# Second attention: x's sum for six of eight batches moved from VectorE to GpSimd

## The reference, cut to what matters

```python
# x = x + _L1_xattn_ref(_layernorm(x), ctx, ctx, Wq, Wk, Wv, Wo)
q = (queries @ Wq).reshape(b, s, KV_HEADS, GROUP, HEAD_DIM)      # 8, 4, 16
k = (keys @ Wk).reshape(b, s, KV_HEADS, HEAD_DIM)
v = (values @ Wv).reshape(b, s, KV_HEADS, HEAD_DIM)
scores = jnp.einsum('bqhgd,bkhd->bhgqk', q, k) * scale
attn = jax.nn.softmax(scores, axis=-1)
out = jnp.einsum('bhgqk,bkhd->bqhgd', attn, v)
return out.reshape(b, s, EMBED) @ Wo
```

## Time and profile before

| | us |
|---|---|
| median of 3 runs (lowest, highest) | 1831.98 (1831.41, 1835.54) |
| profiled execution, its own time | 1834.82 |
| its span, first to last instruction | 1833.1 |
| TensorE busy in the span | 1771.9 |
| VectorE busy | 1412.0 |
| ScalarE busy | 664.4 |
| GpSimd busy | 661.2 |
| mean granted TensorE clock | 0.992 of full |
| six batches of the loop, 1004.4 to 1084.1 | 79.7 |

### The profile page before, as it was taken

The page is one execution under the profiler, slowest core; times in us unless marked ns, Lnnn a source line. Parts: engine busy times, 40 slices in busy tenths (PEclk is TensorE's granted clock), DMA queues, the critical chain, the costliest instruction groups (busy, mean ns, idle before and its releaser), DMA issues. The chain is left out here.

```text
span 1833.1 us, 29590 instructions
## 1 busy us (share of the span) xinstructions
PE 1771.9 (97%) x10246; PEld 1503.6 (82%) x10246; DVE 1412.0 (77%) x2869; ACT 664.4 (36%) x1810; POOL 661.2 (36%) x447
## 2 busy tenths in 40 slices
PE   8999999999999999998998998899999999999998
PEld 6888899889888898896876764685888888888886
DVE  7767777777777777777547966888878888888886
ACT  5432232233331231234046765630443433343333
POOL 6633333444433433433121003544432433243331
PEclk9999999999999999999999998999999999999999
DMA  4111101011111111111023212020110111011011
GB/s 175 63 52 51 50 23 51 31 51 51 51 51 51 39 34 41 41 45 40 22 57 95 64 34 69 23 65 11 37 46 24 46 34 34 23 37 43 24 35 46
DMA packets 45034, 85.35 MB, mean 47 GB/s; under 512 B 5968, under 2 KB 23568, under 8 KB 44592
## 3 DMA queue, kind: packets, MB, share of 16 engines
q1 hardware_dynamic: 44976, 84.59, 14.7%
HBM read 75.39 MB, written 2.10 MB: 42 GB/s over the span
## 5 line engine op out<-in xcount | busy, mean ns | idle before, releaser
L658 POOL TENSOR_TENSOR l0x_comb<-l0x_neg,l0x_bias 128x1024 f32<-128x1024 bf16 x32 | 70.1, 2191 | 370.8 <-DVE l0x_probs L1061 358.6
L953 ACT ACTIVATE l0x_probs_t<-bank 128x512 f32<-128x512 f32 x32 | 19.1, 597 | 494.1 <-PE bank L795 494.1
L2959 POOL TENSOR_TENSOR l3x_q<-l3x_q,l3x_cross 128x512 f32<-128x512 f32 x64 | 89.8, 1408 | 188.0 <-DVE l3x_q L1920 188.0
L37 PE MATMUL bank<-l0x_w_v_hi,ctx_hi 128*128 128x256 f32 x512 | 144.9, 283 | 0.0
L39 PE MATMUL bank<-l0x_w_v_hi,ctx_lo 128*128 128x256 f32 x512 | 144.9, 283 | 0.0
L38 PE MATMUL bank<-l0x_w_v_lo,ctx_hi 128*128 128x256 f32 x512 | 144.9, 283 | 0.0
L937 ACT ACTIVATE l0x_probs<-l0x_probs,l0x_top 128x129 f32<-128x129 f32 x256 | 99.4, 391 | 49.4 <-DVE l0x_top L1067 49.4
L3146 ACT ACTIVATE l3x_probs<-l3x_probs,l3x_top 128x128 f32<-128x128 f32 x256 | 99.1, 389 | 38.1 <-DVE l3x_top L3227 38.0
L37 PE MATMUL bank<-ctx_hi,l0x_w_k_hi 128*128 128x512 f32 x256 | 104.0, 406 | 8.0 <-DVE ctx_lo L1145 8.0
L1107 DVE TENSOR_TENSOR x<-x,bank 128x512 f32<-128x512 f32 x120 | 82.0, 683 | 37.6 <-PE bank L39 37.6
L37 PE MATMUL bank<-l3x_qin_hi,l3x_w_q_hi 128*128 128x512 f32 x256 | 105.8, 413 | 2.2 <-ACT l3x_v L3180 1.9
(11 more groups left out here) (486 smaller groups left out, 5307.0 us busy)
## 6 DMA issues: line engine op xcount, KB each, us to landing
l0x_raw_k<-L_k_dram SPq DMA_DIRECT2D x32, 256.0 KB, 3.4
l0x_raw_v<-L_v_dram SPq DMA_DIRECT2D x16, 512.0 KB, 3.3
l0x_raw_q<-L_q_dram SPq DMA_DIRECT2D x16, 512.0 KB, 4.3
l0x_raw_o<-L_o_dram SPq DMA_DIRECT2D x16, 512.0 KB, 3.4
l3x_raw<-L_q_dram SPq DMA_DIRECT2D x16, 512.0 KB, 3.3
l3x_raw<-L_o_dram SPq DMA_DIRECT2D x16, 512.0 KB, 3.2
kv_raw<-L_kv_dram SPq DMA_DIRECT2D x8, 512.0 KB, 3.4
l1x_stack<-ctx_hi SPq DMA_DIRECT2D x56, 64.0 KB, 2.1
```

Source lines behind the costliest of these rows:

```text
L37: pe.matmul(out, lhs[0], rhs[0], start=start, stop=False)
L658: pool.tensor_tensor(comb[:, :, :], neg[:, :, :], bias[:, j:j + 1, :].to_broadcast([P, B, P]), ALU.add).then_inc(comb_ready, 1)
L953: act.activation(probs_t[:, 0:BH, :], bank[6][:, :].rearrange("p (b n) -> p b n", b=BH), ACT.Copy).then_inc(t_act, 1)
L2959: pool.tensor_tensor(dst[:, part], dst[:, part], cross[n][:, :], ALU.add).then_inc(rotated, 1)
```

## The change

For the first six batches, ScalarE copies bank 7 to a new tile `projected` (two slots in SBUF) behind the exponential of phase 3, and raises `copied`. GpSimd adds that tile to x and raises `o_done`. TensorE's second half of the value product waits for `copied` instead of `o_done` in batches 1 to 6. VectorE takes the statistics of batch b-1 in phase 0 of batch b, behind the division, once `o_done` says that x is there. ScalarE's copy waits for the sum of two batches before, whose slot it takes.

```diff
+    BY_POOL = B - 2
+        projected, copied = sb("projected", [P, 2, D]), sem("copied")
...
                 pool.wait_ge(q_full, 2 * G)
-                ffn.gpsimd(pool)
+                def add_out(b):
+                    pool.wait_ge(copied, b + 1)
+                    pool.tensor_tensor(x[:, b, :], x[:, b, :], projected[:, b % 2, :], ALU.add).then_inc(o_done, 1)
+                ffn.gpsimd(pool, add_out, BY_POOL)
...
-                    wait(pe, at_done if h == 0 else o_done, b)
+                    wait(pe, at_done if h == 0 else copied if b <= BY_POOL else o_done, b)
...
+                def copy_out(b):
+                    act.wait_ge(o_full, b + 1)
+                    wait(act, o_done, b - 1)
+                    act.activation(projected[:, b % 2, :], bank[7][:, :], ACT.Copy).then_inc(copied, 1)
...
                     act.activation(probs[u % 2][:, :, :], probs[u % 2][:, :, :], ACT.Exp).then_inc(exp_done, 1)
+                    if u >= 9 and (u - 9) % G == 0:
+                        copy_out((u - 9) // G)
                     if u >= 5 and (u - 5) % G == 0:
                         copy_values((u - 5) // G)
...
                         if phase == 0:
                             divide(b)
+                            if b >= 1:
+                                dve.wait_ge(o_done, b)
+                                ffn.norm.spread(dve, b - 1)
                         if phase == 1:
                             result_low(b)
-                        if phase == 3:
-                            add_out(b)
...
-    def gpsimd(self, pool):
+    def gpsimd(self, pool, add_first, by_pool):
         pool.memset(self.ones[:, :], 1.0).then_inc(self.ones_done, 1)
         for b in range(B):
+            if b < by_pool:
+                add_first(b)
             self.norm.root(pool, b)
```

## The result

The changed kernel takes 1843.53 us (median of 11 runs, 1842.16 to 1845.51), the kernel before 1833.49 us in 11 runs of the same comparison (1830.84 to 1842.42). The ratio is 1.0054, with an interval of 1.0046 to 1.0063: about 10 us slower (8.4 to 11.6). Forecast were 10.5 us and 1842.5 us.

The account below looks back on a forecast made before the run. VectorE was taken as the bound, with TensorE deciding once per batch through bank 7. Late release 0.93 plus moved statistics 0.82 gave 1.75 us, times six 10.5, on 1831.98: 1842.5 us, range 1838.5 to 1847.

Parts of the forecast that it names:

- The bound: Second attention pass: VectorE sets the pace, except once per batch, at unit 0, where TensorE does, 0.1 us apart.
- rival "faster": Unit 0 doesn't wait for bank 7, so VectorE's sum decides: 0.71 us less per batch, 4.3 us, 1827.7 us; chance 0.04.
- The release of bank 7: Value product's second half waits for ScalarE's copy behind unit 3's exponential: 0.93 us later per batch, bounds 0.9 to 1.1.
- The spared 1.53 us do nothing: Addition and statistics leaving VectorE before unit 0's maxima gain nothing; VectorE then stands idle some 2.6 us.
- The moved statistics: Behind the next batch's division on VectorE, they cost their whole 0.82 us per batch; bounds 0 to 0.82.
- The lower bound of 0: Low limit for the moved statistics' cost per batch, if VectorE waited at unit 1 anyway.
- rival "statistics free": VectorE waits at unit 1 anyway, so only the late bank release costs: 5.6 us, 1837.6 us; chance 0.08.
- GpSimd: Its sum into x, median 1.29 us, ends before the statistics start, with at least 2.2 us of cover.
- The sum: Late release plus moved statistics, 0.93 + 0.82 = 1.75 us per batch, six batches: 10.5 us, giving 1842.5 us.
- The clock: TensorE's clock stays 1.00 in the stretch although it is busy only 83%; a fall would show the prediction wrong.
- the rival with 0.05: TensorE's clock falls in the loop; one batch wholly at 1.2 GHz gives 1852 us, more than one more; chance 0.05.
- The rule on a saturated VectorE: Skill's advice that handing work from saturated VectorE to ScalarE or GpSimd may pay; predicted not to hold at unit 0.

Follow-up runs that it names:

- e5: The kernel before without VectorE's first six additions of the output product to x, nothing waiting for them: 1831.17 us, ratio 0.9994 to the kernel before.
- e1: The kernel before plus a ScalarE copy behind unit 3's exponential, for which the value product's second half also waits: 1838.34 us, ratio 1.0031 to the kernel before.
- e3: The changed kernel with ScalarE's copy of bank 7 ahead of unit 3's exponential instead of behind it: 1837.89 us, ratio 1.0026 to the kernel before.
- e2: The kernel before with only the statistics moved behind the next batch's division, addition left on VectorE: 1838.09 us, ratio 1.0025 to the kernel before.
- e6: The changed kernel with two more sums on GpSimd ahead of each sum into x: 1843.29 us, ratio 1.0059 to the kernel before.
- e7: The changed kernel with four more sums on GpSimd ahead of each sum into x: 1854.70 us, ratio 1.0118 to the kernel before.
- e4: The changed kernel with the copy ahead of unit 3's exponential and statistics between unit 0's maxima and subtraction: 1830.80 us, ratio 0.9993 to the kernel before.

## Why the prediction was right

*The bound.* Right: TensorE through bank 7 and VectorE were 0.1 us apart at unit 0. e5 is the test: with the addition gone VectorE just waits longer. One thing under the rival "faster" was wrong: it held that VectorE's sum decides once bank 7 is free by 1031.6, 0.1 us earlier. In e5 nothing holds bank 7, and VectorE still waits 0.64 us at unit 0: behind the bank comes TensorE's own queue (both halves of the value product, then the transposes), which ends only 0.29 us earlier than before.

*The release of bank 7.* Forecast 0.93 us, measured 0.98 to the subtraction of unit 0. The copy was shorter (0.58 us for 0.60), and TensorE's weights came 0.11 us after its end instead of 0.05. e1 shows the step alone, e3 that the place behind the exponential is its whole cause: ahead of it the same copy brings the subtraction of unit 0 to 3.81 us, as without any addition (e5).

*The spared 1.53 us do nothing.* Right: VectorE waits 2.71 us at unit 0, forecast some 2.6.

*The moved statistics.* 0.82 us in full, as forecast, and 0.80 alone in e2. The lower bound of 0 and the rival "statistics free" are refuted.

*GpSimd.* The sum has 1.27 us and is covered by 3.3 us, where I had at least 2.2; e6 and e7 fix the point from which it decides.

*The sum.* 1.75 us per batch forecast, 1.79 measured. From the subtraction of the first unit 3 to that of the last unit the two profiled executions take 74.14 and 85.38 us, 11.24 more: 6 x 1.79 = 10.74, and 0.5 that one fall of the clock costs, in the period that is 15.56 instead of 15.07. Their spans differ by only 8.3 us. Ahead of this stretch the changed kernel is 0.7 us later, and behind it the kernel before takes 3.7 us longer. There its clock fell at 1105 to 1110 (0.66) and 1320 to 1330 us (0.96 and 0.70) and the changed kernel's, about 10 us later, did not; these three windows make up to 3.4 us, an estimate from the missing share of the clock. So the two spans are no clean measure, and the medians, 10.0 us apart, are the better one. The 1842.5 us are 1.0 off: the kernel before came out 1.5 us above the median that they start from, and the difference 0.5 below the forecast. The 3 us taken for the spread of its runs were small; its first three runs already span 4.1.

*The clock.* The sum has no fall of the clock in it, and the prediction lists one as a sign of being wrong. In the profiled execution there was one: the rival with 0.05 came true in a small form, not a whole batch at 1.2 GHz but part of one, and its 0.5 us are too little to move the result. Windows of the changed kernel:

```profile
1050.00:1055.00 5.00, 3.94 (x33) 2.22 (x34) 2.28 (x3) 3.33 (x4) 1.27 (x1) 1.00 0.00 0
1055.00:1060.00 5.00, 3.46 (x30) 2.95 (x28) 4.70 (x8) 2.82 (x5) 1.06 (x3) 1.00 0.33 80
1060.00:1065.00 5.00, 5.00 (x21) 4.20 (x22) 4.29 (x5) 3.97 (x5) 0.00 (x0) 0.66 0.34 82
```

TensorE was busy 3.46 of 5 us ahead of the fall. e3 has a like one in the loop (its third and fourth period are 14.32 and 14.73), and e7 one in every batch but the first, with TensorE busy 1.52 and 1.32 of 4 us ahead of the two shown. The Trainium skill, "TensorE: Matmul & The Clock Gate", What's actually happening, has the throttled clock as the default which activity lifts. e7 fits this, as its clock fell behind stretches with little work on TensorE, at 0.2 to 0.5 us per batch.

*The rule on a saturated VectorE* (the Trainium skill, "Perfetto Trace Analysis", Optimizing Scalar/DVE Operations) holds here only in part: with nothing added elsewhere (e5) 41% of the time taken off VectorE came through, and with the real copy and sum in the order of e4 the same 0.29 us per batch. In the order of the changed kernel the hand-over cost 1.79 us per batch.

## What to carry to other kernels

Where two engines are each over 90% busy, look for the one instruction per round at which the slower engine already waits, however short that wait: work taken off just ahead of it mostly turns into a longer wait (here 0.43 of 0.71 us). A buffer's release is a step of the path like any other, so when its reader moves to another engine, what stands ahead of the reader in that engine's list counts as much as how long the reader takes: here the copy is shorter than the addition was (0.58 and 0.68 us), and the bank came free 0.98 us later. And work that is put off should be put into a wait, not behind it: between the maxima and the subtraction of unit 0 the statistics were free, three instructions later (behind the subtraction and the division) they cost their full length.

## What the runs showed of the hardware that I had not expected

TensorE's clock can fall in a loop that keeps TensorE busy 83% of the time: 0.66 of full in one window of 5 us of the changed kernel, after windows with 3.94 and 3.46 of 5 us busy and, in the order of time, at most 1.26 us idle before a matmul and 1.94 us before a weight load. It fell in the loop of the changed kernel and of e3, not in those of e1, e2 and e6 with periods between 14.08 and 15.07. e6 has the period of the changed kernel, and in the changed kernel itself another window with 3.46 of 5 us busy (1040 to 1045 us) was not followed by a fall. So at this share it differs from batch to batch and from one execution to another; what decides it stays open.

A sum of one SBUF tile with itself on GpSimd took 1.04 us for 128x512 fp32, a sum of two tiles 1.27 us.
